# GRU recurrence: candidate and update gate multiplied together, in two halves of the units

## The reference

```
def cell(h, x):
    gi = x @ W_ih + b_ih
    gh = h @ W_hh + b_hh
    i_r, i_z, i_n = jnp.split(gi, 3, axis=-1)
    h_r, h_z, h_n = jnp.split(gh, 3, axis=-1)
    r = jax.nn.sigmoid(i_r + h_r)
    z = jax.nn.sigmoid(i_z + h_z)
    n = jnp.tanh(i_n + r * h_n)
    h_new = (1.0 - z) * n + z * h
    return (h_new, h_new)
_, hs = jax.lax.scan(cell, initial_state, xs)
```

## Time and profile before

| | |
|---|---|
| Time, median of 3 runs | 1963.13 us (1960.36 to 1968.94) |
| Profiled execution, span from first to last instruction | 1963.7 us |
| Two attention layers and the products ahead of the loop | about the first 944 us |
| 256 steps of the recurrence | 943.8 to about 1907 us |
| Steps with pieces, in the middle | 213 in 800 us, 3.756 us each |
| Last layer | about the last 57 us |
| PE clock granted in the recurrence | 1.00 |

### The profile page before, as it was taken

How to read it: one execution, slowest core, us unless ns; L and a number is a source line. 1 busy time by engine, 2 the same in 40 slices (tenths; PEclk the granted TensorE clock), 3 DMA queues, 4 the chain that set the end, 5 groups by cost and what they waited for, 6 DMA issues and landing times. The chain is left out here.

```text
span 1963.7 us, 85507 instructions
## 1 busy us (share of the span) xinstructions
PE 1832.6 (93%) x37682; PEld 1269.7 (65%) x37682; DVE 1147.7 (58%) x3364; ACT 785.3 (40%) x2196; POOL 393.5 (20%) x862
## 2 busy tenths in 40 slices
PE   6999999999999999988999999999999999999983
PEld 2433444453444344444998888888888999888861
DVE  5667676766676667343455555555555555555567
ACT  0554565655555565633222222222222222222224
POOL 0121211121111212110122122221222211222113
PEclk7997999999999999989999999999999999999995
DMA  6654443526152623141100000000000000000002
GB/s 160 219 141 126 121 127 85 152 63 181 47 172 67 180 68 93 34 152 42 77 15 10 13 13 13 13 4 13 13 13 13 7 11 13 13 13 12 5 4 86
DMA packets 65377, 127.65 MB, mean 65 GB/s; under 512 B 15401, under 2 KB 22057, under 8 KB 61412
## 3 DMA queue, kind: packets, MB, share of 16 engines
q1 hardware_dynamic: 61372, 120.30, 21.3%
q0 software_dynamic: 3072, 0.82, 0.2%
q10 hardware_dynamic: 560, 1.05, 0.2%
HBM read 77.56 MB, written 37.85 MB: 59 GB/s over the span
## 5 line engine op out<-in xcount | busy, mean ns | idle before, releaser
L439 DVE TENSOR_REDUCE mx<-MX 128x1 f32<-128x512 f32 x768 | 483.3, 683 | 191.7 <-PE MX L568 191.2
L1003 PE MATMUL gate<-whh,state 128*8 128x128 f32 x16384 | 503.8, 273 | 31.5 <-DVE state L919 13.4
L504 ACT ACTIVATE pr<-ST 128x512 f32<-128x512 f32 x768 | 409.5, 596 | 223.5 <-PE ST L588 223.1
L1003 PEld LDWEIGHTS gate<-whh,state 128*8 128x8 f32 x16384 | 430.4, 91 | 87.6 <-DVE state L919 84.7
L896 DVE STREAM_TRANSPOSE trn<-gate 128x128 f32<-128x128 f32 x256 | 81.3, 318 | 337.7 <-PE gate L1003 337.7
L1003 PE MATMUL pg<-whh,state 128*8 128x128 f32 x8192 | 278.4, 273 | 0.3 <-issue 0.3
L951 ACT ACTIVATE rg<-pre 128x32 f32<-128x32 f32 x256 | 58.8, 230 | 504.0 <-DVE pre L898 504.0
L568 PE MATMUL MX<-K,Q 51*128 51x512 f32 (+1 forms) x768 | 242.4, 445 | 15.0 <-DMA Q<-d_q 10.5
L588 PE MATMUL ST<-Q,K 53*128 53x512 f32 (+1 forms) x768 | 240.6, 485 | 13.3 <-ACT pr L504 9.2
L588 PEld LDWEIGHTS ST<-Q,K 53*128 53x128 f32 (+1 forms) x768 | 98.7, 189 | 215.5 <-ACT pr L504 118.9
L1003 PEld LDWEIGHTS pg<-whh,state 128*8 128x8 f32 x8192 | 230.3, 90 | 1.2 <-issue 0.9
(11 more groups left out here) (190 smaller groups left out, 1943.3 us busy)
## 6 DMA issues: line engine op xcount, KB each, us to landing
d_q<-hi_q SPq DMA_DIRECT2D x32, 256.0 KB, 3.5
d_q<-lo_q SPq DMA_DIRECT2D x32, 256.0 KB, 4.0
d_k<-hi_k SPq DMA_DIRECT2D x32, 256.0 KB, 2.9
d_k<-lo_k SPq DMA_DIRECT2D x32, 256.0 KB, 2.9
K<-d_k SPq DMA_DIRECT2D x64, 128.0 KB
Q<-d_q SPq DMA_DIRECT2D x64, 128.0 KB
K<-d_k SPq DMA_DIRECT2D x16, 512.0 KB
Q<-d_q SPq DMA_DIRECT2D x16, 512.0 KB
```

Of the source, the lines that this page charges most:

```text
L439: dve.reduce_max(mx[:, u, col:col + 1], bank[:, :], AX.X).then_inc(mx_red, 1)
L504: act.activation(pr[:, kc % 2, i], ST[n % 3][:, :], ACT.Exp, scale=SCALE[UNITS[w][0]]).then_inc(exped, 1)
L1003: last = pe.matmul(bank[32 * j:32 * j + B, lo:hi], held[q][:, c, :], whh[:, c, o + lo:o + hi], start=first, stop=done)
```

## The change

The weights W_hh get another order of columns, made once ahead of the launch: the reset gate as before, and then, for each half of the units, 64 columns of the candidate beside 64 of the update gate in each of four blocks. So the bank `psA` (`gate1`) holds candidate and update gate of the first half, and `psB` (`pg0`, `pg1` in turns) those of the second half. DVE turns each bank as a whole, once. The candidate's product with r, its sum with the share, the tanh and the scan are done once for each half. The update gate's sigmoid reads the turned tile in SBUF.

```
-                    for c in range(H):
-                        products(psR, R, q, c, c == 0, False)
-                    products(psN, N, q, 0, False, False)
+                    products(psR, 0, q, NEAR, first=True)
+                    products(psA, 1, q, NEAR)
                     if t > 0:
                         pe.wait_ge(s_h[1], t)
...
+                    products(psR, 0, q, FAR, done=True).then_inc(s_psr, 1)
+                    products(psA, 1, q, FAR, done=True).then_inc(s_ps[0], 1)
+                    products(psB[q], 2, q, range(C), done=True).then_inc(s_ps[1], 1)
                     if t + 1 < T:
-                        begin(t + 1)
+                        begin(t + 1, 0)
+                        begin(t + 1, 1)
```

`begin` is called once for each half. Each call waits for the turning of its own bank and issues four matmuls of 64 columns for the bias and four of 64 columns for the shares:

```
+                    if t > a:
+                        pe.wait_ge(s_tr[a], t - a)
                     for j in range(4):
+                        o = P * j + HW * a
+                        pe.matmul(bank[32 * j:32 * j + B, 0:HW], ones_b[:], bnp[:, o:o + HW], start=True, stop=False)
...
+                        pe.matmul(bank[32 * j:32 * j + B, HW:P], pick[:, B * (v % 4):B * (v % 4) + B], foldZ[:, n % RZ, v // 4, o:o + HW], start=False, stop=False)
```

DVE's order after the reset gate, and ACT's loop over the halves:

```
+                    def candidate(a):
+                        dve.wait_ge(s_tr[a], t + 1)
+                        if a == 0:
+                            dve.wait_ge(s_r, t + 1)
+                        dve.tensor_tensor(tmp[:, half(a)], tr[a][:, 0:H], rg[:, half(a)], ALU.mult).then_inc(s_chain, 1)
+                        dve.wait_ge(s_chain, 2 * t + a + 1)
+                        dve.tensor_tensor(pre[:, 1, half(a)], tmp[:, half(a)], share(t, N)[:, half(a)], ALU.add).then_inc(s_pre[a], 1)
...
+                    turn(0)
+                    candidate(0)
+                    turn(1)
+                    update(0)
+                    candidate(1)
+                    update(1)
...
                     for z in range(2):
+                        a.wait_ge(s_tr[z], t + 1)
+                        a.activation(by[:, half(z), :, 2], tr[z][:, H:C], ACT.Sigmoid).then_inc(s_z[z], 1)
+                        a.wait_ge(s_pre[z], t + 1)
+                        a.activation(sides[q][:, half(z), :, 0:3:2], pre[:, 1, half(z)].rearrange("p c (b v) -> p c b v", v=1).to_broadcast([P, H, B, 2]),
+                                     ACT.Tanh).then_inc(s_n[z], 1)
```

More of the change, by code:

```diff
@@ L745, in recurrent_and_last_layer, with half_bank @@
         s_z0 = sem("first_shares_ready")
[L746 to L751, removed]
+        R, N = 0, 1
+        s_psr, s_ps = sem("reset_products"), [sem(f"half_products{a}") for a in range(2)]
+        s_trr, s_tr = sem("reset_turned"), [sem(f"half_turned{a}") for a in range(2)]
+        s_prer, s_pre = sem("reset_summed"), [sem(f"candidate_summed{a}") for a in range(2)]
+        s_n = [sem(f"candidate_ready{a}") for a in range(2)]
         s_z = [sem(f"update_ready{a}") for a in range(2)]
         s_h = [sem(f"state_ready{a}") for a in range(2)]
-        psR, psN, zb = ps
+        psR, psA, zb = ps
+        psB = pg[0:2]
         NINIT = 22
-        tR, tN = 0, 1
+        HW = P // 2
+        def half_bank(a, t):
+            return psA if a == 0 else psB[t % 2]
         TG, TZ, RZ = 16, 16, 3
@@ L913, in _, with turn @@
-                    for a in range(2):
+                    dve.wait_ge(s_psr, t + 1)
+                    dve.transpose(trn[:, 2, :], psR[:, 0:P]).then_inc(s_trr, 1)
+                    dve.wait_ge(s_trr, t + 1)
+                    dve.tensor_tensor(pre[:, 0], tr[2], share(t, R), ALU.add).then_inc(s_prer, 1)
+                    def turn(a):
+                        dve.wait_ge(s_ps[a], t + 1)
+                        dve.transpose(trn[:, a, :], half_bank(a, t)[:, 0:P]).then_inc(s_tr[a], 1)
@@ L998, in _, with products @@
                 pe.wait_ge(s_init, NINIT)
-                def products(bank, g, q, c, first, done, lo=0, hi=P):
-                    for j in range(4):
[L1002 to L1013, removed]
+                def products(bank, part, q, chunks, first=False, done=False):
+                    for c in chunks:
+                        for j in range(4):
+                            o = part * D + P * j
+                            last = pe.matmul(bank[32 * j:32 * j + B, 0:P], held[q][:, c, :], whh[:, c, o:o + P], start=first and c == chunks[0], stop=done and c == chunks[-1])
+                    return last
@@ new lines, in begin @@
+                def begin(t, a):
+                    n, v = t // TZ, t % TZ
+                    bank = half_bank(a, t)
+                    if a == 0:
+                        if t == 0:
+                            pe.wait_ge(s_z0, 1)
+                        elif n > 0 and v == 0:
+                            pe.wait_ge(s_zd[n % RZ], 192 * (n // RZ + (0 if n % RZ == 0 else 1)))
+                    if t > a:
+                        pe.wait_ge(s_tr[a], t - a)
+                    for j in range(4):
+                        o = P * j + HW * a
+                        pe.matmul(bank[32 * j:32 * j + B, 0:HW], ones_b[:], bnp[:, o:o + HW], start=True, stop=False)
@@ L1014, in begin @@
                     for j in range(4):
+                        o = P * j + HW * a
                         if n == 0:
[L1016 removed]
+                            pe.matmul(bank[32 * j:32 * j + B, HW:P], identz[:, B * v:B * v + B], giZ[0][:, o:o + HW], start=False, stop=False)
                             continue
[L1018 removed]
@@ L1019, in begin @@
[L1019 to L1023, removed]
+                        pe.matmul(bank[32 * j:32 * j + B, HW:P], pick[:, B * (v % 4):B * (v % 4) + B], foldZ[:, n % RZ, v // 4, o:o + HW], start=False, stop=False)
+                begin(0, 0)
+                begin(0, 1)
+                NEAR, FAR = range(H), range(H, C)
```

58 lines of the change are left out of this document (16 added, 42 removed).

## The result

The changed kernel is slower: 2029.85 us, the median of four runs (2028.62 without the slowest), against 1963.87 us for the kernel before in the same session; the ratio is 1.0326, with a 95% interval of 1.0291 to 1.0362. The profiled execution took 2028.62 us with a span of 2026.8, which is 63.1 more than before. The forecast was 33 more.

What follows compares the result with a forecast made beforehand. The prediction took PE's instruction supply, in blocks of 256 records, as the limit: 1963.7 us, +30 for the middle steps, +5 for the first 16, -2 for the last 16, together 1997 us; range 1922 to 2048, if slower 1978 to 2048.

Steps and rivals of the forecast that it cites:

- The chain: Latencies from a step's first set to the next step's state: 3.58 us forecast against 3.71, 0.13 less.
- PE's waits for the state: Sign of a right forecast: PE's waits for the new state nearly vanish in the middle steps.
- PE's own work: Twelve sets, `begin` and the pieces: 3.40 to 3.51 us a step together, hidden inside the chain's 3.58.
- The stream decides: PE's instruction supply in 256-record blocks sets the step: 272 records in place of 256, taken as 3.89 us.
- The rate: Supply of PE's instructions in the middle steps: 70.1 records per us, taken from the first 16 steps.
- term of +30: The 224 middle steps at 3.89 us in place of 3.756: 30 us more.
- The POOL adds: POOL's additions in each step: claimed to keep their place, waiting for the same scan as before; no cost counted.
- the first rival: Supply as fast as a block in 3.37 us, so the chain's 3.58 decides: 1919 us; chance 0.18.
- the blocks keep pace: PE's instruction blocks can come every 3.37 us, so the chain decides: 39 us less in the middle, 1919; chance 0.18.
- the blocks come at their best pace: PE's instruction supply at 3.45 us for 256 records, a step of 3.67 us: 1943 us; chance 0.08.
- The slow pace: PE's instruction supply at 66.4 records per us, a step of 4.10 us: 2048 us; chance 0.17.
- The second half is late: Supply no limit, but the second scan comes 0.93 us behind the first: a step of 3.78, 1969 us; chance 0.07.

Runs made afterwards that it cites:

- merged_half_pool: after_merged_half with POOL's work on the shares cut into halves of 256 columns, one a step, behind its wait for the new state: 1946.83 us, ratio 0.9890.
- after_whole: The changed kernel with each piece in the loop as one matmul over 128 rows in place of four over 32, 236 records a step: 1977.46 us, ratio 1.0050.
- after_merged: The changed kernel with bias and shares in one tile, so one matmul of 2 x 64 columns starts a bank, 256 records a step: 1981.03 us, ratio 1.0070.
- before_split: The kernel before with begin's bfloat16 matmuls in halves of 64 columns, 272 records a step, chain untouched: 2013.97 us, ratio 1.0214.
- after_merged_half: after_merged with pieces of two matmuls over 64 rows in place of four over 32, 232 records a step: 1969.54 us, ratio 1.0016.
- before_dense: The kernel before with 1280 matmuls of 8 columns added ahead of the first step, waiting for nothing and never read: 2000.01 us in one run.
- after_pool: The changed kernel with only POOL's work on the shares cut into halves of 256 columns and placed behind its wait for the state: 2028.33 us, ratio 1.0306.

## Why the prediction was right in sign and short in size

The direction, the mechanism and the range held; the time was 33 us too low. By the prediction's steps:

- **The chain** was right: 3.58 forecast, 3.56 in a step without a stop. No version runs at it in the mean; merged_half_pool comes nearest with 3.665. That it doesn't set the changed kernel's step is shown by after_whole and after_merged, where the step falls from 4.01 to 3.81 and 3.78 as records are taken out and the order of work stays. One sign that the prediction named came only in part: PE's waits for the state did not nearly vanish, they fell by half, from 63.1 us in 168 to 30.2 in 93.
- **PE's own work** was hidden, as said, but the cover is thin: in the step shown the last loads of the pieces end at 1130.79 and the state comes at 1130.86. All of `begin` lies inside, so its small matmuls cost the step no time but that of their records. after_whole is the case in which that cover is gone.
- **The stream decides** was right, and is shown from both sides: records added to the kernel before slow it (before_split), records taken from the changed kernel end the stops (after_whole, after_merged_half), and before_dense has the pace, with the packets that make it, and nothing else in the way. The count of 272 was right, too: the page's 2112 matmuls more are eight a step.
- **The rate is the step that failed.** The sum took 70.1 records per us for the middle, because the first 16 steps had more than a block a step as well; the middle ran at 67.9. So its term of +30 measured +58, and the 16 first steps cost +7 in place of +5. The last 16 gave 2 back, as forecast. The rate wasn't one number: the changed kernel itself has 69.1 (4,437 records in 64.20 us) at the beginning and 67.9 later, and before_split 68.8. A value between the 70.1 and the 66.4 of the earlier trace rows would have been the better choice: at 68, a step is 4.00.
- **A cost that was put at nothing.** The POOL adds were to keep their place, since "they wait for the same scan as before". They do wait for the same scan, the second one, but that now comes 0.90 us behind the first, so within a step the adds come some 0.7 us later and meet DVE's sum. In the changed kernel stops cover it (after_pool); in after_whole, after_merged and after_merged_half they don't. Had the stream been fast, it would have taken some 24 us of the first rival's gain.

Of the rivals, "the blocks keep pace" and "the blocks come at their best pace" fell: 3.45 appears again and again in before_dense, but the mean in the recurrence is 3.77. "The slow pace" was nearer than the forecast: 67.9 lies between 70.1 and 66.4, and 2048 is 18 us off where 1997 is 33 off. "The second half is late" fell as the cause, though its sign was there: by the trace PE's loads do wait for the second half ahead of the fifth set in 125 of 216 middle steps, but for 0.12 us each, 15 us in all, and in after_whole and after_merged the step fell with that order unchanged.

Why a block takes 3.45 us in one place and 3.7 to 4.0 in another is answered in part by the packets: in before_dense, with no engine but PE at work, a longer block has a longer packet. Open stays what makes a packet longer, and what fills the 1.1 us ahead of it and the 1.3 behind it; nothing was tried on either.

## What to carry to other kernels

Where PE runs many small matmuls, count its instructions as well as its columns: here a float32 matmul is four records and a bfloat16 matmul two, and 256 records cost 3.45 us at best and about 3.8 in the mean in these kernels, however short their work. An edit that splits a matmul is then paid in records, and one that merges two earns them back, until PE's own time for the wider matmuls becomes the limit. When one limit is removed, look through the new chain for instructions that used to have slack: here a sum that met POOL's additions.

## What the runs showed of the hardware

- DVE's sum of two tiles in SBUF took 0.19 us alone and 0.76 beside POOL's addition of 512 columns; with additions of 256 columns placed elsewhere, 0.196 in the mean. The Trainium skill, "SBUF — State Buffer", section "Who interferes with whom", has a DVE instruction with two SBUF inputs contend with a GpSimd instruction that reads SBUF; the trace agrees.
- The supply of PE's instructions is as slow at a granted clock of 1.00 as at 0.50 (1.2 GHz): 3.47 us between two stops 256 records apart in before_split (1037.23 to 1040.70), 3.45 in before_dense.
- Instructions came to PE one block of 16 KB at a time: the next packet started 1.0 to 1.8 us after PE had entered a block, took 0.88 to 1.47, and PE went on 1.2 to 1.6 behind its end (the changed kernel's 112 stops with over 0.5 us between two starts).
- A float32 weight load took 109 ns for 32 columns, 136 for 64 (after_merged_half) and 190 for 128; a matmul over fewer, wider loads is not cheaper for PE, only for the stream.
- The sigmoid of 128x16 on ACT takes 225 ns where it reads the turned tile in SBUF; the kernel before had 193 reading a bank of PSUM. There it lies in the tail (turn, sigmoid, scan); in the changed kernel the first half's is done long before the scan.
